# Keys of tiles 3 to 15 loaded in blocks of 32 channels and turned by VectorE for groups of tiles, in place of TensorE transposes per tile

## The reference, cut to what matters

```python
x: (64, 32, 256); ctx_1024: (64, 257, 256); w_q, w_k, w_v: (256, 1024); w_o: (1024, 256); 16 heads of 64
q = split_heads(layernorm(x) @ w_q); k = split_heads(ctx @ w_k); v = split_heads(ctx @ w_v)
scores = q @ k.T * 64 ** -0.5
scores += (1 - causal_mask) * -10000.0          # key position <= query position stays
out = softmax(scores) @ v
x = x + concat_heads(out) @ w_o
```

## Time and profile before

| | |
|---|---|
| time, median of 3 runs | 584.04 us (582.31 to 585.48) |
| the profiled execution's own time | 583.32 us |
| its span | 581.4 us |
| PE, PEld busy | 536.8, 428.8 us |
| DVE, ACT, POOL busy | 445.5, 234.0, 44.9 us |
| DMA | 31.03 MB, mean 53 GB/s |

### The profile page before, as it was taken

How to read it: one execution, slowest core, us unless ns; L and a number is a source line. 1 busy time by engine, 2 the same in 40 slices (tenths; PEclk the granted TensorE clock), 3 DMA queues, 4 the chain that set the end, 5 groups by cost and what they waited for, 6 DMA issues and landing times.

```text
span 581.4 us, 18921 instructions
## 1 busy us (share of the span) xinstructions
PE 536.8 (92%) x7928; PEld 428.8 (74%) x7944; DVE 445.5 (77%) x867; ACT 234.0 (40%) x477; POOL 44.9 (8%) x83
## 2 busy tenths in 40 slices
PE   4979999999999999999985789999999999999865
PEld 3769888889888888888764667777777777777543
DVE  3728789888889888888850569888888888888852
ACT  1323233323233323332343556555555555555211
POOL 5000100000000000000020111111111111111100
PEclk9989999999999999999987989999999999999987
DMA  8991221112211012222200000000000000000000
GB/s 256 347 280 74 72 72 28 45 72 72 72 72 55 18 72 72 72 72 74 75 3 3 3 3 2 9 9 9 9 9 9 9 9 9 9 9 10 10 9 19
DMA packets 13801, 31.03 MB, mean 53 GB/s; under 512 B 976, under 2 KB 10704, under 8 KB 11728
## 3 DMA queue, kind: packets, MB, share of 16 engines
q1 hardware_dynamic: 13776, 30.67, 15.8%
HBM read 28.57 MB, written 2.10 MB: 53 GB/s over the span
## 4 chain that ended last, share of the span: by engine, by line
PE 49%; issue 29%; DVE 13%; ACT 5%; POOL 3%; POOLq 0%; DVEq 0%; ACTq 0%
PE bank L375 10%; PE bank L397 10%; PE bank L422 9%; PE bank L366 9%; PE bank L413 4%; ACT x_oT L504 2%; DVE f_xn L1398 2%; POOL f_rstd L1091 2%; DVE f_h L1407 1%; PE bank L1182 1%; DVE f_amax_x L1493 1%; DVE f_xn L1532 1%; PE bank L1204 1%; ACT a_kblocks L1306 1%; PE bank L1158 1%
## 5 line engine op out<-in xcount | busy, mean ns | idle before, releaser
L375 PEld LDWEIGHTS bank<-x_xcT,xwk 128*128 128x128 f32 x512 | 61.9, 198 | 2.8 <-issue 1.1
L375 PE MATMUL bank<-x_xcT,xwk 128*128 128x128 f32 x512 | 62.3, 282 | 1.4 <-ACT x_xcT L487 1.4
L397 PE MATMUL bank<-xwv,x_xcT 128*128 128x512 f32 x128 | 59.7, 609 | 1.0
L422 PE MATMUL bank<-xwo,x_oT 128*128 128x256 f32 x256 | 59.7, 388 | 0.8 <-ACT x_oT L504 0.8
L366 PE MATMUL bank<-x_xcT,xwq 128*128 128x128 f32 x512 | 59.8, 275 | 0.0
L366 PEld LDWEIGHTS bank<-x_xcT,xwq 128*128 128x128 f32 x512 | 58.5, 192 | 0.0
L422 PEld LDWEIGHTS bank<-xwo,x_oT 128*128 128x128 f32 x256 | 48.6, 195 | 7.7 <-issue 1.4
L518 ACT COPY x_k_blocks<-bank 64x512 f32<-64x512 f32 x32 | 18.6, 581 | 87.8 <-PE bank L375 87.6
L1158 PE MATMUL bank<-wdT,f_hqT 128*128 128x256 f32 x192 | 47.5, 399 | 4.2 <-DVEq L1423 2.3
L1306 ACT ACTIVATE a_kblocks<-bank,head_rows 128x256 f32<-128x256 f32 x128 | 48.4, 499 | 0.0
L1182 PE MATMUL bank<-wgT,f_xqT 128*128 128x192 f32 (+1 forms) x128 | 42.2, 474 | 3.6 <-DVE f_out L1364 3.6
(11 more groups left out here) (152 smaller groups left out, 938.6 us busy)
## 6 DMA issues: line engine op xcount, KB each, us to landing
x_ctx_slab<-in_ctx_dram SPq DMA_DIRECT2D x16, 1028.0 KB, 4.8
out_dram<-f_out SPq DMA_DIRECT2D x16, 128.0 KB, 1.7
xall<-in_x_dram SPq DMA_DIRECT2D x1, 1280.0 KB, 16.2
x_first_keys<-in_ctx_dram SPq DMA_DIRECT2D x4, 320.0 KB, 12.2
xwk<-in_L_xattn_w_k_dram SPq DMA_DIRECT2D x1, 1024.0 KB, 5.1
xwq<-in_L_xattn_w_q_dram SPq DMA_DIRECT2D x1, 1024.0 KB, 7.1
xwv<-in_L_xattn_w_v_dram SPq DMA_DIRECT2D x1, 1024.0 KB, 10.3
xwo<-in_L_xattn_w_o_dram SPq DMA_DIRECT2D x1, 1024.0 KB, 12.8
```

The costliest lines, as they stand in the source:

```text
L375: last = nc.tensor.matmul(bank[2 + j // 4][:, (j % 4) * P:(j % 4 + 1) * P], xwk[:, k, j * P:(j + 1) * P], xcT[:, KD + k, :], start=(k == 0 ...
L397: last = nc.tensor.matmul(bank45[:, half, :], xcT[:, KD + k, :], xwv[:, k, half * 512:(half + 1) * 512], start=(k == 0), stop=(k == KD - 1))
L422: last = nc.tensor.matmul(bank67[:, 0, 0:D], oT[:, j].rearrange("p b q -> p (b q)"), xwo[:, j, :], start=(j == 0), stop=(j == XP - 1))
```

## The change

The key rows of tiles 0, 1 and 2 (`NAT = 3`) are loaded and turned as before, from a smaller buffer `keys_in_rows`, now read by TensorE directly, without the copy `c_now`. The keys of tiles 3 to 15 come in pieces: a DMA takes 32 channels of all 32 key rows of the batches of a group of tiles to 32 partitions, so that a block of 32 x 32 (row, channel) stands where VectorE's transpose turns it in place of the other. There are three groups (tiles 3 to 5, 6 to 10, 11 to 15; `KPARTS`), each of 8 pieces (`KB`), in rows of 128 bytes. The pieces of the first group are issued behind the feed-forward weights, those of the others in threes, threes and twos behind the slabs 1 to 6. VectorE turns each group with two instructions (`turn_keys`), after the tile steps 1, 4 and 9, to `first_keysT`, and ScalarE copies one tile of it to `xcT` just ahead of its copy of the turned x (`copy_keys`, then `copy_xc`, now half as wide). TensorE's first loop pass is written out, since tile 2 is turned in it by TensorE; ScalarE and VectorE have three loops each in place of one.

```diff
+                NAT = 3
+                c_first = psb("keys_in_rows", [P, NAT, D])
+                crows = psb("first_keys", [P, KD, T - NAT, BT, SQ])
+                call = psb("first_keysT", [P, KD, T - NAT, BT, SQ])
...
+                NPARTS, KPARTS = ((0, 1), (1, NAT)), ((NAT, 6), (6, 11), (11, T))
...
+                    def load_keys(part, n):
+                        t0, t1 = KPARTS[part]
+                        k, g = n // (P // 32), n % (P // 32)
+                        at = k * P + g * 32
+                        sp.dma_start(crows[g * 32:(g + 1) * 32, k, t0 - NAT:t1 - NAT, :, :],
+                                     ctx_blocks[0:SQ, t0:t1, :, at:at + 32]).then_inc(s_c[part], 16)
...
+                    for n in range(KB):
+                        load_keys(0, n)
...
-                    with sp.Fori(1, T) as t:
+                    for t in range(1, 7):
+                        sp.wait_ge(s_slu, t)
+                        load_slab(t)
+                        for n in range((t - 1) % 3 * 3, min((t - 1) % 3 * 3 + 3, KB)):
+                            load_keys(1 + (t - 1) // 3, n)
+                    with sp.Fori(7, T) as t:
...
                     def turn(t):
                         pe.wait_ge(s_xn, t + 1)
-                        pe.wait_ge(s_cn, t + 1)
...
+                        if isinstance(t, int) and t < NAT:
+                            pe.wait_ge(s_c0[0 if t == 0 else 1], 16 * BT)
+                            for k in range(KD):
+                                last = nc.tensor.transpose(bank[1][:, (KD + k) * P:(KD + k + 1) * P],
+                                                           c_first[:, t, k * P:(k + 1) * P], ident[:])
                         last.then_inc(s_t, 1)
...
+                    def copy_keys(t, parts):
+                        act.wait_ge(s_cn, parts)
+                        act.wait_ge(s_v, t)
+                        nc.scalar.copy(xcT[:, KD:, :],
+                                       call[:, :, bass.ds(t - NAT, 1)].rearrange("p k o b i -> p k (o b i)"))
...
+                    def turn_keys(part):
+                        t0, t1 = KPARTS[part]
+                        dve.wait_ge(s_c[part], 16 * KB)
+                        for k in range(KD):
+                            last = nc.vector.transpose(call[:, k, t0 - NAT:t1 - NAT].rearrange("p t b i -> p (t b i)"),
+                                                       crows[:, k, t0 - NAT:t1 - NAT].rearrange("p t b i -> p (t b i)"))
+                        last.then_inc(s_cn, 1)
...
                     tile_step(1, True, True, True, True, False)
+                    turn_keys(0)
                     row_statistics(2)
...
-                    with dve.Fori(W0, T - 2) as t:
-                        tile_step(t, True, True, True, True, True)
+                    for t0, t1 in ((W0, 5), (5, 10), (10, T - 2)):
+                        with dve.Fori(t0, t1) as t:
+                            tile_step(t, True, True, True, True, True)
+                        if t1 < T - 2:
+                            turn_keys(1 if t1 == 5 else 2)
```

More of the change, by code:

```diff
@@ L198, in psb @@
                     return st1.enter_context(nc.sbuf_tensor("x_" + name, shape, dt))
[L199 removed]
+                NAT = 3
+                c_first = psb("keys_in_rows", [P, NAT, D])
+                crows = psb("first_keys", [P, KD, T - NAT, BT, SQ])
+                call = psb("first_keysT", [P, KD, T - NAT, BT, SQ])
                 stats, mv = psb("ln_stats", [P, T, 6]), psb("ln_mv", [P, T, 2])
                 ve, rstd = psb("ln_ve", [P, T]), psb("ln_rstd", [P, T])
[L202 removed]
+                xn = psb("xn", [P, D])
                 xcT = psb("xcT", [P, 2 * KD, P])
@@ L226, in cross_attention @@
                 s_x = [sem(f"x_part{i}_loaded") for i in range(len(PARTS))]
-                s_c = [sem(f"keys_part{i}_loaded") for i in range(len(PARTS))]
+                s_c = [sem(f"keys_part{i}_loaded") for i in range(len(KPARTS))]
+                s_c0 = [sem(f"key_rows_part{i}_loaded") for i in range(len(NPARTS))]
                 s_qw, s_kw, s_vw, s_ow = sem("wq_loaded"), sem("wk_loaded"), sem("wv_loaded"), sem("wo_loaded")
@@ L352, in turn @@
                         pe.wait_ge(s_xn, t + 1)
-                        pe.wait_ge(s_cn, t + 1)
                         for k in range(KD):
[L355 to L358, removed]
+                            last = nc.tensor.transpose(bank[1][:, k * P:(k + 1) * P], xn[:, k * P:(k + 1) * P],
+                                                       ident[:])
+                        if isinstance(t, int) and t < NAT:
[3 more added lines that the diff above has]
+                                                           c_first[:, t, k * P:(k + 1) * P], ident[:])
                         last.then_inc(s_t, 1)
@@ L443, in pe_program, with tile_step @@
                     pe.wait_ge(s_ow, 16)
-                    with pe.Fori(0, T - 2) as t:
+                    def tile_step(t):
                         project_k(t + 1)
@@ L451, in pe_program @@
                         output(t)
+                    tile_step(0)
+                    with pe.Fori(1, T - 2) as t:
+                        tile_step(t)
                     project_k(T - 1)
@@ L486, in copy_xc @@
                         act.wait_ge(s_t, t + 1)
-                        nc.scalar.copy(xcT[:], turned(bank[1][:])).then_inc(s_tc, 1)
+                        if isinstance(t, int) and t < NAT:
+                            nc.scalar.copy(xcT[:], turned(bank[1][:])).then_inc(s_tc, 1)
+                        else:
+                            nc.scalar.copy(xcT[:, 0:KD, :], turned(bank[1][:, 0:D])).then_inc(s_tc, 1)
                     def copy_q(t):
@@ L532, in act_program @@
                     copy_v(0)
[L533 to L549, removed]
+                    spread_k(1)
+                    copy_q(1)
+                    copy_o(0)
+                    exp(1)
+                    copy_v(1)
+                    copy_xc(2)
+                    for part, (t0, t1) in enumerate(KPARTS):
+                        with act.Fori(t0 - 2, t1 - 2) as t:
+                            spread_k(t + 1)
+                            copy_q(t + 1)
+                            copy_o(t)
+                            exp(t + 1)
+                            copy_v(t + 1)
+                            copy_keys(t + 2, part + 1)
+                            copy_xc(t + 2)
                     spread_k(T - 1)
```

19 lines of the change are left out of this document (9 added, 10 removed).

## The result

The changed kernel took 576.99 us (median of 4 runs, 574.59 to 578.1) beside 584.75 (4 runs) for the kernel before on the same chip: a ratio of 0.9869 [0.9822, 0.9916]. On another chip it took 577.62 (6 runs, 574.85 to 580.76) beside 584.4 (14 runs), 0.9884 [0.9848, 0.9920]. By the medians it is faster by 7.8 and 6.8 us. The forecast was 582.1, its range began at 579: the prediction was wrong, and too careful. The profiled execution took 577.9, span 576.2, against 583.32 and 581.4.

What follows compares the result with a forecast made beforehand. The prediction took TensorE's program order to bound the kernel: -2.8 (transposes) + 0.85 (first group) = -1.95 us, so 581.4 for the profiled execution and 582.1 us as forecast, range 579 to 586.

Steps and rivals of the forecast that it cites:

- I take no change: TensorE's first-pass wait for code, 3.03 us plus 1.33 at the lower clock: stays as it was, 0 us.
- -4.4 (gone): Favourable end for TensorE's first-pass hole: 3.03 + 1.33 us vanish; a smaller hole as rival had chance 0.17.
- the queue is not empty before some 40 us: Argument against the first-pass hole shrinking: the DMA queue stays filled past the code fetch.
- about 31 us: DMA queue: time when the loads ahead of the first group of key pieces end.
- Transposes, 13 x 0.22, "I take -2.8": TensorE, tiles 3 to 15: two key transposes fewer per tile, 0.22 us each tile, -2.8 us in all.
- The first group, "0.85 once": VectorE's turn ahead of the row statistics delays the residual add; TensorE waits 0.85 us at `project_q(3)`, bounds 0.6 to 2.0.
- The later groups, ScalarE's copies, the landing of the pieces, "nothing": VectorE's 1.8 us turns, ScalarE's key copies and the pieces' DMA all stay hidden within the room: 0 us.
- Packets of 128 bytes, "30 ns": DMA of key pieces: each packet takes 30 ns, bounds 6 and 89; landing hidden at either bound.
- The rival of slow packets: Small DMA packets at 178 ns; first group lands at 65.4, TensorE stands 11 us: 594 us; chance 0.07.
- A second fetch hole "at 50 to 60 us": TensorE waits for code in the new loop's first pass, up to 3.0 + 1.3 us: typically 584; chance 0.14.
- from -4.4 to +2: Bounds for TensorE's first-pass hole: gone, or a code fetch behind slower packets; 0 was taken.

Runs made afterwards that it cites:

- before, first pass out: Kernel before the change, with only TensorE's first loop pass written out as in the changed kernel: 585.44 us against 584.73, ratio 1.0017.
- changed, old load back: Changed kernel, with the old load of key rows of tiles 6 to 15 added into a buffer nobody reads: 580.57 us against 584.15, ratio 0.9958.
- before, keys late: Kernel before the change, with the key rows of tiles 6 to 15 issued behind all weights: 583.26 us against 584.15, ratio 0.9971.
- changed, pieces behind: Changed kernel, with the first group's eight key pieces issued behind the self-attention weights: 578.76 us against 584.4, ratio 0.9911.
- before, queue held: Kernel before the change, SP waiting for tile 1's projected values before issuing key rows of tiles 6 to 15 and all behind: 580.93 us against 584.73, ratio 0.9946.
- the changed kernel again: Changed kernel, unaltered, run once more on another chip: 577.62 us against 584.4 for the kernel before, ratio 0.9884.
- transposes put back: Changed kernel, with two further transposes in each of TensorE's 13 loop passes: 581.67 us against 584.15 for the kernel before, ratio 0.9946.
- group turned behind the statistics: Changed kernel, first group of keys turned after VectorE's row statistics, TensorE's stand at tile 3 gone: 578.74 us against 584.15, ratio 0.9888.
- from tile 2: Changed kernel, key blocks from tile 2, no TensorE pass written out, first group turned after VectorE's tile step 0: 576.28 us against 584.73, ratio 0.9862.

## Why the prediction was wrong, step by step

**The step that failed** is "I take no change" for the hole in TensorE's first pass. Its cause was read rightly (waiting for code behind a full DMA queue), and the end of the range that applies, "-4.4 (gone)", was worked out rightly: 3.03 + 0.83 + 0.50 (the ledger has 4.6, since the last matmuls of `weigh(0)` ran at the lower clock too). What was wrong is the argument against it, "the queue is not empty before some 40 us". It added up bytes and packets for the data queue and never asked when SP can issue them. Its "about 31 us" for the end of the older loads was right. But SP spends 9.02 us on eight issues, from 24.77 on, and these 3072 packets are worth only 192 x 14 ns = 2.7 us of each DMA engine. The queue runs dry at 31.5 us while SP still issues, the code comes 4.8 us earlier (31.55 instead of 36.31), and TensorE has it before it needs it. That SP's issues can take up to 4.5 us stood in the profile of before; how long pieces of many small packets take did not.

The table gives, from the traces, when TensorE begins the second `project_q`, when the transfer of the piece of code begins, and until when the hole lasts (us):

| data queue while the code comes | `project_q` | code | code later by | hole, until |
|---|---|---|---|---|
| before, full (104%) | 30.47 | 36.31 | 5.8 | 3.03, 38.59 |
| before, first pass out, 104% | 29.82 | 35.33 | 5.5 | 2.84, 37.78 |
| changed, old load back, 106% | 29.78 | 34.18 | 4.4 | 1.82, 36.71 |
| before, keys late, 104% | 29.87 | 34.13 | 4.3 | 1.70, 36.67 |
| changed, pieces behind, 123% | 30.19 | 33.72 | 3.5 | 1.08, 36.39 |
| before, queue held, empty | 30.62 | 32.06 | 1.4 | none |
| changed, just run dry | 29.70 | 31.55 | 1.9 | none |

The holes follow the time at which the code comes, counted from the same place in TensorE's work, in either program. The four other runs without an early hole (the changed kernel again, transposes put back, group turned behind the statistics, from tile 2) have 1.2 to 1.4 us in the fourth column. TensorE goes on 2.3 to 2.7 us after the piece has begun to come, in all five holes. Behind the holes of 1.70 us and more the granted clock fell to its lower level (L386 and its like at 1.73 to 1.94 us), behind 1.08 it did not. So the clock's part is not in proportion: none once, and 1.3 to 2.7 us in L386 and L397 and their like the other four times.

**Transposes, 13 x 0.22, "I take -2.8":** right. The tile is 17.04 us, the ledger has -2.5 over twelve tiles, and putting them back costs 0.6% of 584 = 3.4 us against the kernel with the stand removed, where 2.8 and the stand were to be expected.

**The first group, "0.85 once":** right in place and releaser, a little large: the starts of L405 and L396 lie 4.14 us apart at 60.53 and 64.67 where 3.57 is usual, and 0.10 more stood before L405: 0.67. The two turns of 384 columns took 1.04 us (1.05 foreseen), the longest of those of 640 columns 837 ns (0.87 foreseen). The view of the instruction:

```profile
L667 DVE STREAM_TRANSPOSE x_first_keysT<-x_first_keys x6: 537/801/837, 48.6 to 190.8; 128x640 f32<-128x640 f32 x4, 128x384 f32<-128x384 f32 x2
```

**The later groups, ScalarE's copies, the landing of the pieces, "nothing":** right. Among TensorE's waits after there is none for them behind tile 3; ScalarE's copy of the keys takes 0.41 us and its half copy 0.38; no VectorE idle time ends with a DMA of keys (one of 2.9 us ends with that of `xwk`, as before); the pieces land within 2.8 to 6.6 us.

**Packets of 128 bytes, "30 ns":** 14 by the row above, inside the bounds of 6 and 89, but the value taken was twice too high, and it made the queue look longer than it is. This alone would not have shown the dry queue: at 14 ns the weights would still stand right behind the pieces, had SP issued them in time. The rival of slow packets falls.

**A second fetch hole "at 50 to 60 us":** wrong place. The new loop's first pass has none. There is one at `scores(15)`, behind the loop, where I had not looked: a piece of code begins to come at 274.46 us, and the last matmul of `scores` waits until 276.85. Written out, the first pass shifts all code behind it; that this brings the hole is shown by the kernel before with that edit alone (1.38 us at the same place) and by the version from tile 2, which has neither. That TensorE waits for this piece is argued, not shown: it goes on 2.2 to 2.8 us after the piece has begun to come in all seven profiled executions with this hole, close to the 2.3 to 2.7 of the early holes. The full queue is not the cause there, since no data moved between 270 and 274.4 us in the changed kernel; the piece comes late for another reason, which stays open.

**The sum.** -4.4 (hole) - 2.8 + 0.67 + 0.7 (second hole, net) = -5.8 us; the spans of the two profiled executions differ by 5.2, those of the repeat by 5.1 (581.4 to 576.3). The ledger closes the gap between the two: -0.2 more for the hole, -0.77 ahead of it, +1.5 behind `output(15)`. The medians say -7.8 and -6.8, with intervals that reach to -4.9 and -4.7. The granted clock falls several times in each execution behind 294 us, at places that differ: before from 294.4 over L422 of the last tile (5.41 us, against 3.69 after), after at 309.8 over work that ran at full speed before. The windows of these stretches (busy us of PE, PEld, DVE, ACT, POOL, then PEclk, DMA share, GB/s), before and after:

```profile
294.40:297.80 3.40, 3.40 (x9) 2.67 (x9) 2.23 (x19) 0.00 (x0) 0.95 (x1) 0.51 0.03 7
```

```profile
309.80:316.60 6.80, 6.34 (x75) 4.68 (x71) 2.09 (x3) 1.88 (x5) 0.00 (x0) 0.50 0.00 0
```

The four executions of the changed kernel had a mean clock of 0.982 at 574.59 and 576.08 us and of 0.976 at 577.9 and 578.1; the profiled one is of the latter, and so is that of the kernel before (0.976). So the profiled pair leaves out what the medians have of the clock. Over the 62 executions of the kernel before that ran beside the experiments the mean clock is 0.973 and never above 0.976; over the ten of the changed kernel it is 0.978, four of them at 0.982. Among the 62, those at 0.971 took 585.1 us in the median and those at 0.976 took 582.5, so 0.005 of the clock go with 2.7 us. Of the 0.005 between the two means, 0.003 are the fall behind the early hole (3.4 us at half the clock), which the sum has already; the rest is worth an estimated 1.3 us, and the missing 1 to 2 us have that size. Why the clock falls less often elsewhere in the changed kernel was not tried.

## What to carry to other kernels

An idle time that ends with "issue" shortly after a piece of code has come in can be a wait for that code, and the code can stand behind a full DMA queue: price a change by what the queue holds at that moment, and count for this both the time of the packets and the time in which they can be issued. Small pieces that are slow to issue can leave a queue emptier than few large ones. But look whether the queue is full at all; the second hole here came beside an empty one. A term whose bounds reach from -4.4 to +2 must be decided by working out that one moment, not by taking the middle; and if an edit writes out code, look for idle time on "issue" at every later place where many short instructions follow each other.

## What the runs showed of the hardware

A packet of 128 bytes to 32 partitions took 14 ns to move. SP needed 1.1 us in the mean (0.47 to 1.98) to issue a DMA of 384 such rows, most of them while older loads filled the queue, and 0.62 us for one of 640 rows later; four DMAs of 1 KB rows took 9.60 us to issue behind a full queue and 1.84 us into an empty one. A transpose by VectorE in 32x32 blocks took 537 and 579 ns for 384 columns, 700 for 512 and 801 to 837 for 640. A fetch of a 16 KB piece of code beside a full data queue stopped TensorE for 1.08 to 3.03 us; in the same place, with the queue empty or just run dry, it stopped it not at all. Elsewhere, beside an idle queue, TensorE still stood 1.12 to 1.71 us on "issue" after such a piece.
